# Two graph layers on one core: one more group of softmax tiles turned by VectorE, and the counts of the next graph's adjacency in later slots

## The reference

```
# layer 0
h = max(layernorm(x), 0)
Q, K, V = h Wq^T + bq, h Wk^T + bk, h Wv^T + bv        # 8 heads of 32
s = where(adj == 0, -inf, Q K^T / sqrt(32));  p = softmax(s)
x = x + (p V) Wo^T + bo
# layer 1
h = max(layernorm(x), 0)
e_k = leaky_relu((h * a_k) h^T, 0.2)                   # k = 0..3
s = where(adj == k + 1, e_k, -9e15);  x = x + softmax(s) h
```

## Time and profile before

| what | value |
|---|---|
| median of 3 runs | 3588.59 us (3587.13 to 3589.55) |
| the profiled execution | 3593.83 us |
| its span, first to last instruction | 3592.0 us |
| mean granted clock of TensorE | 0.977 |
| one pass of the loop | 212.1 to 214.7 us |

### The profile page before, as it was taken

How to read it: one execution, slowest core, us unless ns; L and a number is a source line. 1 busy time by engine, 2 the same in 40 slices (tenths; PEclk the granted TensorE clock), 3 DMA queues, 4 the chain that set the end, 5 groups by cost and what they waited for, 6 DMA issues and landing times. The chain is left out here.

```text
span 3592.0 us, 96785 instructions
## 1 busy us (share of the span) xinstructions
PE 3252.4 (91%) x32304; PEld 2698.2 (75%) x32304; DVE 2823.2 (79%) x5398; ACT 2447.6 (68%) x4548; POOL 1112.3 (31%) x568
## 2 busy tenths in 40 slices
PE   5789989999998999989999998999999899998975
PEld 4567878777787887778777787877778788787854
DVE  4668888787888878888887888878888887888752
ACT  4666776767677677766767677676767767776641
POOL 1142333324233242422324233332423324242222
PEclk8899999999999999999999999999999999999988
DMA  5754646565464755646476464746546475564501
GB/s 132 208 134 143 174 128 195 131 190 158 132 180 123 217 134 163 166 127 181 129 210 157 141 172 123 203 126 191 159 138 179 123 216 134 162 167 122 150 30 41
DMA packets 331134, 546.84 MB, mean 152 GB/s; under 512 B 44481, under 2 KB 209601, under 8 KB 328385
## 3 DMA queue, kind: packets, MB, share of 16 engines
q1 hardware_dynamic: 330432, 538.36, 54.5%
HBM read 286.53 MB, written 134.22 MB: 117 GB/s over the span
## 5 line engine op out<-in xcount | busy, mean ns | idle before, releaser
L879 DVE CUSTOM_DVE_ANT_0 sm<-ps,bias 128x1024 f32<-128x1024 f32 x1024 | 1245.9, 1217 | 75.1 <-issue 31.0
L604 ACT ACTIVATE sm<-sm,mn 128x1024 f32<-128x1024 f32 x1024 | 1179.2, 1152 | 83.5 <-DVE mn L879 82.5
L1229 PE MATMUL pT<-ident,sm 128*128 128x128 f32 x6400 | 856.8, 276 | 83.8 <-ACT pt L615 76.4
L1229 PEld LDWEIGHTS pT<-ident,sm 128*128 128x128 f32 x6400 | 726.5, 141 | 258.4 <-ACT pt L615 123.0
L531 POOL TENSOR_SCALAR gbias<-adj_half 128x512 bf16<-128x512 int32 x256 | 492.7, 1925 | 1338.2 <-DVE mn L1002 971.3
L615 ACT COPY pt<-pT 128x512 f32<-128x512 f32 x784 | 456.1, 582 | 544.4 <-PE pT L1229 530.6
L1217 PE MATMUL ps<-ks,qs 96*128 96x512 f32 x2048 | 747.2, 446 | 81.9 <-DVE mn L879 78.3
L514 POOL TENSOR_SCALAR bias<-adj_half 128x512 bf16<-128x512 int32 x256 | 492.2, 1923 | 681.5 <-DMA adj_half<-in_adj_dram 588.0
L903 DVE COPY pt<-pT 128x512 f32<-128x512 f32 x560 | 384.1, 686 | 206.5 <-PE pT L1229 196.5
L1248 PE MATMUL pG<-pt,v 128*32 128x128 f32 x16128 | 510.8, 278 | 30.0 <-DVE pt L903 19.6
L1248 PEld LDWEIGHTS pG<-pt,v 128*32 128x32 f32 x16128 | 440.6, 111 | 106.3 <-issue 91.1
(11 more groups left out here) (106 smaller groups left out, 3695.8 us busy)
## 6 DMA issues: line engine op xcount, KB each, us to landing
adj_half<-in_adj_dram SPq DMA_DIRECT2D x512, 256.0 KB, 4.1
bounce<-turned SPq DMA_DIRECT2D x896, 128.0 KB, 2.5
pt<-bounce SPq DMA_DIRECT2D x224, 512.0 KB, 4.6
ks<-parts SPq DMA_DIRECT2D x384, 128.0 KB, 2.6
qs<-parts SPq DMA_DIRECT2D x384, 128.0 KB, 2.8
x<-in_x_dram SPq DMA_DIRECT2D x16, 1024.0 KB, 5.7
out_dram<-x SPq DMA_DIRECT2D x128, 128.0 KB, 4.6
wqk<-ks SPq DMA_DIRECT2D x60, 256.0 KB, 7.5
```

Source lines behind the costliest of these rows:

```text
L604: nc.scalar.activation(sm[:, ring(t), :], sm[:, ring(t), :], ACT.Exp, scale=-1.0, bias=mn[:, t:t + 1], accum_out=den[:, t:t + 1]).then_inc ...
L879: nc.vector.tensor_tensor_reduce(out=sm[:, ring(t), :], in0=ps[t % 2][:, :], in1=bias[:, node, :], scale=1.0, scalar=3e38, op0=ALU.add, op ...
L1229: last = nc.tensor.transpose(pT[c][:, j * P:(j + 1) * P], sm[:, ring(t), m * P:(m + 1) * P], ident[:, :])
```

## The change

SWAPPED becomes groups 3 to 10 instead of 3 to 9, so tiles 40 and 41 are turned by DVE and moved by SP. By the constants, the values product of group 10 moves from the end of slot 44 to slot 46 ahead of its transposes; ASIDE moves from tile 41 to 45; edge row 6 becomes LATE and row 7 SPARED, so row 7's edge values move from slot 45 to 46 and row 6's are spread over slots 42 to 44. The result of row 7 is put one slot later by hand. MOST, the slots of the counts of nodes 0 to 6, is 46, 48, 51, 53, 56, 59, 62 instead of 43, 46, 48, 51, 55, 58, 61. On SP the blocks of group 10 are moved behind the store of row 4; the weights are put back ahead of the load of node 0 instead of behind it. The edge rows, the front transposes and the products of keys and queries keep their slots otherwise.

```diff
-SWAPPED = tuple(range(3, 10))
+SWAPPED = tuple(range(3, 11))
...
-MOST = (43, 46, 48, 51, 55, 58, 61)
+MOST = (46, 48, 51, 53, 56, 59, 62)
...
-    return EDGE + 1 + 4 * NT if t == NT - 1 else EDGE + (8 if t in LATE else 7) + 4 * t
+    return EDGE + 2 + 4 * NT if t == NT - 1 else EDGE + (8 if t in LATE else 7) + 4 * t
...
                 swap_blocks(b, 9)
                 store(o, 4)
+                swap_blocks(b, 10)
                 if later:
+                    restore(b)
                     mask_adj(b + 1, 0, base)
-                    restore(b)
                 store(o, 5)
...
                     swap_blocks(0, 9)
+                    swap_blocks(0, 10)
                     restore(0)
```

## The result

The changed kernel takes 3681.20 us (median of 4 runs, 3678.37 to 3699.56); the kernel before took 3589.07 beside it (4 runs). The ratio is 1.0262, with a 95% interval of 1.0247 to 1.0277: 2.6% slower. The forecast was 3640, with 3600 to 3666 as the range: the sign is right, the size too small by 41 us, and the time lies outside the range.

The account below looks back on a forecast made before the run. No engine is simply full; the wait that ends last in each slot bounds it. Fourteen passes losing 4.9 and gaining 1.0 us, less 2 and 1.5 for first and last, give +51: about 3640 us, range 3600 to 3666.

Parts of the forecast that it names:

- The turn: Slots 40 to 47: turning group 10 gains 1.0 us a pass, bounds 0 and 2.9, its DMAs all hidden.
- My walk through the slots: Following PE and DVE from slot 40 to the next graph's key product, which comes at about 1489.6 instead of 1490.56.
- my fourth rival: Slots 40 to 47: the turn gives nothing because DVE's order takes it all; 3656 us; chance 0.12.
- The Trainium skill's rule: Read weight loads, not matmul busy time: 13.02 of 16.41 us in slots 40 to 43, so the gain could be nothing.
- The later counts: ACT's adjacency counts in later slots delay load 4 behind load 3 and the key copies; 4.9 us lost a pass.
- the term of 4.9 us a pass: Loss from ACT waiting 3.5 us for load 4 at slot 56, exp of slot 57 5.4 later; bounds 3.4 and 7.1.
- Its chain: On SP after count 2: load 3, twelve key copies taking 8.90 us, load 4, landed for ACT 5.17 later.
- The slow clock (third rival): PE idling around slot 57 drops the granted clock to 1.2 GHz: up to 1.7 us more a pass, 3664; chance 0.13.
- The sum: 14 middle passes at 4.9 - 1.0 (+54.6), first pass -2, last -1.5: +51 us, about 3640.
- First and last pass: First: the 5.8 us load wait at slot 46 goes, -2 in all; last: the turn alone, -1.5.
- The signs that I named: 6144 PE transposes, 256 turns, ACT idle some 70 us, load 3 to load 4 back to back, slots 40-47 1 us shorter.
- the signs that I am wrong: Load 4 issued over 6 us before its count's slot, key copies under 8 us, or slots 40-47 3 us shorter.

Follow-up runs that it names:

- counts later, hardly a wait (54, 58, 63): Changed kernel with counts in slots 46, 48, 51, 54, 58, 61, 63 and PE's program padded by empty steps (32 + 33): 3594.82 us, 0.9999.
- the counts alone: Kernel before with only the counts moved to slots 46, 48, 51, 53, 56, 59, 62, group 10 not turned: 3684.88 us, 1.0271.
- holding the clock up: Changed kernel with 16 unread PE transposes added ahead of the transposes of tiles 55 and 58: 3653.82 us, 1.0168.
- the filled-up changed kernel: Changed kernel with PE's program padded by empty steps, 32 ahead of the loop and 33 in a never-taken branch: 3665.92 us, 1.0196.
- The turn that looked 1.5% slower: Group 10 turned, counts in their old slots, node 0's load ahead of group 10's blocks on SP, no padding: 3646.55 us, 1.0154.

## Why the prediction was wrong in size

The ratios make an account, each entry the difference of two of them, times 3590:

```
turn of group 10, count out of slot 43        0.9950 - 1           -18 us   forecast -16
counts later, hardly a wait (54, 58, 63)      0.9999 - 0.9950      +18  |
counts 3 to 6 at 53, 56, 59, 62 instead       1.0196 - 0.9999      +71  |   forecast +67
PE's wait at the loop's turn                  1.0262 - 1.0196      +24      forecast none
all                                                                +94      forecast +51
```

The entries hang on the order in which they are taken, and each is good to 5 to 8 us by the intervals: the counts alone cost +97 on the kernel before, which has no wait at the turn, and the turn then takes off 27 (1.0196 - 1.0271) and not 18. Why the second entry is 18 was not followed further than to its slots.

- **The turn: right.** -1.0 us a pass in slots 40 to 47, to the tenth, with the DMAs of group 10 and the put-back of the weights hidden as said (PE and its weight loads wait 5.0 us for the blocks over the span, 3.6 before). What I missed is that the gain hangs on the move of count 0: with the count left in slot 43 it is nothing (0.9998). My walk through the slots nowhere has that count, so the right size is in part luck. So my fourth rival, that the turn gives nothing, is true of the turn with that count and false of the change. The Trainium skill's rule, which pointed to it (Perfetto Trace Analysis, "Identifying the Most-Contended Engine"), is borne out by the one version and not by the other; the row of weight loads could not tell them apart.
- **The later counts: right in kind, too small by 22 us.** The step that failed here is the term of 4.9 us a pass. Its chain held: from the end of count 2 to count 4 I had 16.0 us, measured 15.46; to load 4 10.9, measured 10.21; key copies 8.90, measured 8.26 (7.55 to 9.66); the wait at slot 53 1 to 2, measured 1.63. But I let that wait pass through ACT as if only ACT lost it. PE has nothing else to do in slots 53 to 55, so it stands 2.36 us a pass ahead of tile 55's transposes, slows down, delivers values 13 late, and ACT comes to count 4 2.4 us later than I had it (14.89 for 12.5 us behind the end of count 2). Hence a wait of 0.57 us for the forecast 3.5, and yet a larger loss: slots 48 to 60 +5.8 a pass for +4.9. With the waits taken away four fifths of the loss go (71 of 89 us). (By its own rows the chain is 1.9 us shorter than before, not 2.1; nothing hangs on it.)
- **The slow clock (third rival): it came, and is not what it was priced at.** I gave it 1.7 us a pass on top. It is there in 12 of 14 passes; holding the clock up was worth some 10 us in all, since load 4 sets when count 4 starts. The stretch of the earlier trace rows that I took it from is not slots 12 to 15: by the masks, counted as for slots 40 to 47, it is slots 16 to 19.
- **The sum: it lacked a term, and this is the other step that failed.** Nothing in the prediction looks at how many instructions PE's program has. The 33 fewer a pass and 32 fewer ahead of the loop put the jump back at a bad place, a cost that the sum has at nothing: 24 us here, 55 to 58 us where ACT's stalls don't cover it. With it gone the changed kernel takes 3665.92, just inside the end of my range; with it, it is outside.
- **First and last pass: right in sign** (-3.9 and -2.3 for -2 and -1.5); what makes up the difference was not followed.
- **The signs that I named:** 6144 transposes and 256 turns, as said. Load 4, the copies and load 3 back to back, as said. ACT's idle time at the counts 42.6 us for 70: wrong, by the point above. Slots 40 to 47 about 1 us shorter, as said. Of the signs that I am wrong one did come, in half of the passes: the key copies took under 8 us in 7 of 14 (7.56 in the rows above).

One thing stays open: some +1.1 us a pass around the loop's turn in the filled-up changed kernel. Count 6, moved from slot 61 to 62, stands there, and slot 60 is 0.6 shorter for it; the rest comes in passes with half clock at the masks of tiles 2 and 3. It was not tried apart.

## What to carry to other kernels

Follow a wait through to the engine that will have nothing to do: 1.6 us of ACT's waiting in slot 53, where PE had no other product, made slot 55 3.3 us longer, while about the same wait (1.56) in slot 55 of before, with a values product on PE meanwhile, left PE idle 0.66 us. When an edit changes the number of instructions in a loop, look at the first instruction behind each jump for idle time marked "issue", and compare with a version filled up by empty steps before the edit itself is judged: the turn that looked 1.5% slower was level with before (0.9991) with 32 such steps, and 0.5% faster with its count in another slot. A change of two parts is best timed as two: here one part was good and hidden under the other.

## What the runs showed of the hardware

- PE waits 3.1 to 3.7 us for instructions behind the loop's jump back at one place of the program (3.25 in the row above), 2.0 us on the mean behind a skipped branch of 128 steps (28.4 us in 14 passes), and not at all at others; a 16 KB packet of q8 lands 1.25 to 2.15 us ahead of the end of each of these waits. The kernel's time varies by 1.6% with nothing but 32 empty steps ahead of the loop (1.0154 to 0.9991).
- Behind an idle stretch of 1.85 us in slot 55, PE's next eight transposes took 1.97 us for 1.04, and the granted clock of that slot was 0.70 of 2.4 GHz.
- The load of node 3 takes 4.7 us from the issue of its first half to the landing of the second in the changed kernel, and 6.75 us in the one before, where it goes out three slots earlier. Why was not tried.
